# First convolution's stage: the nodes' leaky rows are made on VectorE, and their own rows are added there from SBUF

## The reference

```
x = _layernorm(x + _L0_gnn_ref(x, edge_index, ...))                   # graph convolution, twice, 64 -> 128 -> 64
x = _layernorm(x + _L1_gnn_ref(x, src, dst, ...))                     # attention over the edges
x = _layernorm(x + _L2_gnn_ref(x, edge_attr_64, ..., edge_type_10))   # relations; ends as below
x = _layernorm(x + _L3_gnn_ref(x, src, dst, edge_attr_32, ...))       # messages and an update MLP
```

```
out = leaky_relu((nfeat + h_nb) @ res_fc_w.T, 0.01) + leaky_relu(nfeat * h_nb @ res_fc2_w.T, 0.01)
x   = layernorm(x + out)
```

## Time and profile before

| | |
|---|---|
| median of 3 runs | 4774.9 us (4772.15 to 4782.6) |
| profiled execution: its own time | 4780.41 us |
| profiled execution: span of the trace | 4778.7 us |
| granted TensorE clock, mean over the span | 0.884 |
| first convolution's stage in the span | about 859 to 1422 us, 98 turns |

### The profile page before, as it was taken

One profiled execution on the slowest core, in us unless ns is written; L12 is line 12 of the kernel. 1 busy time (PEld: TensorE's weight loads), 2 busy tenths in 40 slices (PEclk: granted clock), 3 DMA queues, 4 the chain that ended last, 5 costly groups with the idle time before them and its releaser, 6 DMA issues. The chain is left out here.

```text
span 4778.7 us, 78736 instructions
## 1 busy us (share of the span) xinstructions
PE 4088.1 (86%) x24119; PEld 2923.4 (61%) x24119; DVE 3215.4 (67%) x7115; ACT 1960.7 (41%) x3684; POOL 2801.5 (59%) x2859
## 2 busy tenths in 40 slices
PE   5989999799989999778996899898998666777776
PEld 1278888688877777668884555555555344444443
DVE  9967777667667888767776688888888433333332
ACT  0056666344444445324342155555555222222222
POOL 0066665576656666577762545455550377777777
PEclk9989999899999999855555989999998799888888
DMA  1089998799986676545543444444442222222221
GB/s 40 1 256 286 287 287 270 196 230 230 229 216 171 191 191 188 139 95 136 133 114 86 109 104 110 107 112 107 113 110 53 67 66 66 55 66 67 55 65 29
DMA packets 1127654, 649.03 MB, mean 136 GB/s; under 512 B 908912, under 2 KB 944313, under 8 KB 1127240
## 3 DMA queue, kind: packets, MB, share of 16 engines
q1 hardware_dynamic: 1039432, 555.85, 42.4%
q0 software_dynamic: 87808, 88.16, 9.3%
HBM read 384.70 MB, written 261.63 MB: 135 GB/s over the span
## 5 line engine op out<-in xcount | busy, mean ns | idle before, releaser
L2237 POOL DMA_INDIRECT r_got<-x_table,slot_idx x392 | 409.9, 1046 | 568.5 <-DVE r_masked L2470 340.0
L1089 POOL DMA_INDIRECT o_rows<-in_x_dram,dst_idx x392 | 369.9, 944 | 444.8 <-POOLq L348 242.0
L2552 POOL DMA_INDIRECT m_rows<-x_table,slot_idx x392 | 376.2, 960 | 223.9 <-issue 118.8
L2691 DVE TENSOR_TENSOR_SCAN m_both<-m_keep,m_both,m_rows_t 128x512 f32<-128x512 bf16 x97 | 124.1, 1280 | 545.2 <-PE m_rows_t L2614 545.2
L1541 POOL DMA_INDIRECT b_rows<-h_table,slot_idx x392 | 369.7, 943 | 206.9 <-issue 91.5
L1352 POOL DMA_INDIRECT a_got<-node_table,src_idx x392 | 375.5, 958 | 194.9 <-DVE a_conv L1488 57.4
L2336 PE MATMUL r_source_t<-r_masked,rel_pair 64*128 64x512 f32 x980 | 470.9, 626 | 0.0
L2338 PE MATMUL r_own_t<-r_masked,rel_pair 64*128 64x512 f32 x980 | 470.8, 626 | 0.0
L2560 POOL DMA_INDIRECT out_dram<-s_res,put_out x392 | 390.5, 996 | 135.7 <-issue 109.8
L2010 POOL DMA_INDIRECT t_got<-x_table,slot_idx x392 | 377.5, 963 | 144.8 <-issue 101.2
L2470 DVE SCALAR_TENSOR_TENSOR r_masked<-r_half,r_both_t 128x512 f32<-128x512 bf16 x490 | 301.0, 678 | 68.3 <-PE r_both_t L2321 68.2
(11 more groups left out here) (401 smaller groups left out, 11785.3 us busy)
## 6 DMA issues: line engine op xcount, KB each, us to landing
x_table<-n_res SPq DMA_DIRECT2D x196, 256.0 KB
n_rows<-x_table SPq DMA_DIRECT2D x196, 256.0 KB
x_table<-s_res SPq DMA_DIRECT2D x294, 128.0 KB
node_table<-n_wide SPq DMA_DIRECT2D x98, 272.0 KB, 3.9
h_table<-n_conv SPq DMA_DIRECT2D x98, 256.0 KB
x_table<-s_res SPq DMA_DIRECT2D x98, 256.0 KB
r_feats<-in_edge_attr_dram SPq DMA_DIRECT2D x390, 64.0 KB
n_rows<-in_x_dram SPq DMA_DIRECT2D x97, 256.0 KB
```

The source lines that it names most:

```text
L1089: nc.gpsimd.indirect_dma_start(out=rows[:, n % 4, t, :], out_offset=None, in_=x, in_offset=bass.IndirectOffsetOnAxis(ap=dst_idx[:, n * TIL ...
L2237: nc.gpsimd.indirect_dma_start(out=got[:, n % RING, t, :], out_offset=None, in_=x2_table, in_offset=bass.IndirectOffsetOnAxis(ap=slot_idx[ ...
L2552: nc.gpsimd.indirect_dma_start(out=rows[:, n % 4, t, 0:D], out_offset=None, in_=x3_table, in_offset=bass.IndirectOffsetOnAxis(ap=slot_idx[ ...
```

## The change

In the relations layer only (this stage):

- ScalarE no longer applies ReLU: `take` copies the projected rows from PSUM to a new SBUF tile `n_plain`. Its place in ScalarE's list is that of the old bend. The next projection now waits for this copy.
- VectorE makes the leaky rows: `leak`, one scalar_tensor_tensor max(0.01 y, y) of 128x512, from `n_plain` to `n_hidden`.
- TensorE's `sum_up` keeps one product per group, `cen_pair` with `n_hidden`. The products with `slope_pair` are gone.
- The node's own (already centred) row is added on VectorE: `join_rows` adds `n_rows` from SBUF to the sum in PSUM and writes `n_whole` in SBUF. Squares and the final scaling read `n_whole` instead of PSUM (`squares_joined`, `scale_joined`). Loads of rows now also wait until the block that last held the buffer was joined.
- VectorE's list is in another order.

```diff
         def project(self, pe, n):
             pe.wait_ge(self.copied[n], self.copied.done(n))
             if n >= 1:
-                pe.wait_ge(self.bent[n - 1], self.bent.done(n - 1))
+                freed = self.plain_made if self.layer == "relations" else self.bent
+                pe.wait_ge(freed[n - 1], freed.done(n - 1))
...
                     if self.layer == "relations":
-                        nc.tensor.matmul(to[:, pair(q)], rows_s[:, pair(q)], slope_pair[:, :, :].rearrange("k j d -> k (j d)"),
-                                         start=(q == 0), stop=False, skip_group_check=True)
-                        last = nc.tensor.matmul(to[:, pair(q)], hidden[:, pair(q)], bent_pair[:, :, :].rearrange("k j d -> k (j d)"),
-                                                start=False, stop=True, skip_group_check=True)
+                        last = nc.tensor.matmul(to[:, pair(q)], hidden[:, pair(q)], cen_pair[:, :, :].rearrange("k j d -> k (j d)"),
+                                                start=(q == 0), stop=True, skip_group_check=True)
                         continue
...
+        def take(self, act, n):
+            act.wait_ge(self.projected[n], self.projected.done(n))
+            if n >= 2:
+                act.wait_ge(self.bent[n - 2], self.bent.done(n - 2))
+            nc.scalar.activation(self.plain[:, n % 2, :], self.hidden_t[:, :], ACT.Copy).then_inc(self.plain_made[n], 1)
+
+        def leak(self, dve, n):
+            dve.wait_ge(self.plain_made[n], self.plain_made.done(n))
+            if n >= 2:
+                dve.wait_ge(self.summed[n - 2], self.summed.done(n - 2))
+            nc.vector.scalar_tensor_tensor(out=self.hidden[:, n % 2, :], in0=self.plain[:, n % 2, :], scalar=SLOPE, in1=self.plain[:, n % 2, :],
+                                           op0=ALU.mult, op1=ALU.max).then_inc(self.bent[n], 1)
...
-                    over_turns((bend, 3, BLOCKS), (squares_nodes, 2, BLOCKS), (roots_nodes, 2, BLOCKS), (bend_nodes, 1, BLOCKS),
+                    over_turns((bend, 3, BLOCKS), (squares_nodes, 2, BLOCKS), (roots_nodes, 2, BLOCKS), (take_nodes, 1, BLOCKS),
                                (copy_nodes, 0, BLOCKS))
...
-                    over_turns((powers_nodes, 2, BLOCKS), (scale_conv, 3, BLOCKS), (add_terms, 3, BLOCKS), (invert_nodes, 2, BLOCKS),
-                               (scale_nodes, 2, BLOCKS), (sum_up, 1, BLOCKS), (scale, 0, BLOCKS))
+                    over_turns((join_nodes, 2, BLOCKS), (scale_conv, 3, BLOCKS), (add_terms, 3, BLOCKS), (powers_nodes, 2, BLOCKS),
+                               (leak_nodes, 1, BLOCKS), (sum_up, 1, BLOCKS), (invert_nodes, 2, BLOCKS), (scale_nodes, 2, BLOCKS),
+                               (scale, 0, BLOCKS))
```

More of the change, by code:

```diff
@@ L821, in __init__ @@
                 self.hidden = sb(c, "n_hidden", [P, 2, 512])
-            if layer == "update":
+                self.plain = sb(c, "n_plain", [P, 2, 512])
+                self.plain_made = sig.get("rising")
+            if layer in ("relations", "update"):
                 self.whole = sb(c, "n_whole", [P, 2, ROWS, D])
@@ L846, in load @@
                 sp.wait_ge(self.turned[n - AHEAD], self.turned.done(n - AHEAD))
-            if n >= AHEAD and self.layer == "update":
+            if n >= AHEAD and self.layer in ("relations", "update"):
                 sp.wait_ge(self.joined[n - AHEAD], self.joined.done(n - AHEAD))
@@ L929, in sum_up @@
                 pe.wait_ge(self.bent[n], self.bent.done(n))
-            if self.layer == "update":
+            if self.layer in ("relations", "update"):
                 if n >= 2:
@@ L987, in bend @@
                     act.wait_ge(self.summed[n - 2], self.summed.done(n - 2))
[L988 to L992, removed]
+            nc.scalar.activation(self.hidden[:, n % 2], self.hidden_t[:, :, :], ACT.Relu,
+                                 bias=(b1_col if self.gcn else u_b1)[:, 0:1]).then_inc(self.bent[n], 1)
+        def take(self, act, n):
[9 more added lines that the diff above has]
+                                           op0=ALU.mult, op1=ALU.max).then_inc(self.bent[n], 1)
         def squares(self, act, n):
@@ L1445, in copy_nodes, with take_nodes @@
                         nodes.copy(act, n)
-                    def bend_nodes(n):
-                        nodes.bend(act, n)
+                    def take_nodes(n):
+                        nodes.take(act, n)
                     def squares_nodes(n):
-                        nodes.squares(act, n)
+                        nodes.squares_joined(act, n)
                     def roots_nodes(n):
                         nodes.roots(act, n)
-                    over_turns((bend, 3, BLOCKS), (squares_nodes, 2, BLOCKS), (roots_nodes, 2, BLOCKS), (bend_nodes, 1, BLOCKS),
+                    over_turns((bend, 3, BLOCKS), (squares_nodes, 2, BLOCKS), (roots_nodes, 2, BLOCKS), (take_nodes, 1, BLOCKS),
                                (copy_nodes, 0, BLOCKS))
@@ L1504, in scale_nodes, with leak_nodes, join_nodes @@
                     def scale_nodes(n):
-                        nodes.scale_rows(dve, n)
-                    over_turns((powers_nodes, 2, BLOCKS), (scale_conv, 3, BLOCKS), (add_terms, 3, BLOCKS), (invert_nodes, 2, BLOCKS),
-                               (scale_nodes, 2, BLOCKS), (sum_up, 1, BLOCKS), (scale, 0, BLOCKS))
+                        nodes.scale_joined(dve, n)
+                    def leak_nodes(n):
+                        nodes.leak(dve, n)
+                    def join_nodes(n):
+                        nodes.join_rows(dve, n)
+                    over_turns((join_nodes, 2, BLOCKS), (scale_conv, 3, BLOCKS), (add_terms, 3, BLOCKS), (powers_nodes, 2, BLOCKS),
+                               (leak_nodes, 1, BLOCKS), (sum_up, 1, BLOCKS), (invert_nodes, 2, BLOCKS), (scale_nodes, 2, BLOCKS),
+                               (scale, 0, BLOCKS))
             sig.end_phase()
```

## The result

The changed kernel takes 4825.95 us (median of 3 runs, 4825.89 to 4830.29) against 4774.9 us before: a ratio of 1.0104, 95% interval 1.0084 to 1.0123. It is slower by 51 us, which is clear of the 0.2% that can be told. Measured again beside the experiments, the ratio was 1.0108 (1.0091 to 1.0125).

The account below looks back on a forecast made before the run. TensorE bounds the kernel before at 5.49 us a turn; afterwards a VectorE-ScalarE chain sets 5.99. 97 x (5.99 - 5.486) = +49 us on the profiled 4780.4, less 5.5 for the median, gave 4825 us, range 4803 to 4855.

Parts of the forecast that it names:

- TensorE sets the pace before: Relations stage before the change: TensorE busy 500 of 500 us, its timeline filling the 5.49 us turn without a hole.
- The floors: Least turn after the change: TensorE 4.60 us, gathers 3.8 and something between them, transfers 5.0, VectorE 5.03; all below 5.49.
- The chain: VectorE and ScalarE hand work over twice per turn; VectorE waits 0.96 us before the leak, making the turn 5.99 us.
- TensorE can deliver: TensorE's sums reach VectorE at 4.84 us after the join's start, needed at 5.99; TensorE idles 1.4 us per turn.
- J: Start of the join on VectorE, from which the forecast counts times in a turn, in us.
- The sum: Relations stage: 97 turns x (5.99 - 5.486) = +49 us, giving 4825 us for the median of the runs.
- The rival in which VectorE's queue is full: Wait for the leak hidden, turn 5.03 us: -44 us, 4731; with transfers at 0.91 share, -10 us, 4765. Chance 0.08.
- The clock rival: TensorE's idle time lowers its clock to 1.2 GHz: +30 to +100 us more, 4855 to 4925. Chance 0.08.
- The rule on the most-contended engine: Take the engine with highest occupancy, TensorE at 500 of 500 us, as bottleneck and relieve it first; the change then pays.

Follow-up runs that it names:

- e5: Changed kernel with all sixteen passes on TensorE again, the own row counted twice in the result: 4831.25 us, against 4832.43 for the changed kernel beside it.
- e1: Changed kernel with the copy (`take`) moved ahead of the root in ScalarE's list: 4740.37 us, 0.991 of the kernel before.
- e3: Changed kernel with the copy (`take`) one place later in ScalarE's list, behind the copy of the transposed rows: 4914.28 us, ratio 1.0272 to the kernel before.
- e4: Changed kernel without the leak: ScalarE applies ReLU straight to `n_hidden`, the slope left out; join and eight passes stay: 4741.93 us, 0.991 of the kernel before.
- e7: Kernel before with only the leak moved to VectorE: no join, sixteen passes, squares and scaling from PSUM: 4780.45 us, ratio 0.9998 to the kernel before.
- e2: Changed kernel with the scan moved ahead of the leak in VectorE's list: 4769.98 us, 0.997 of the kernel before.
- e6: Changed kernel with the copy (`take`) behind the copy of the transposed rows and sixteen TensorE passes, own row counted twice: 4888.34 us, ratio 1.0226 to the kernel before.

## Why the prediction was right

The forecast was 4825 us, the chance of slower 0.88, and the time is 4826 us. Step by step:

- **TensorE sets the pace before, and its queue is full.** e5 is the reverse test for after: with the sixteen passes back the time is the same, so after the change TensorE is off the path.
- **The floors are all below 5.49.** Right. VectorE's 5.03 us with no wait was measured as 5.01 in e1. The gathers' 3.8 us "and something between them" was too low a floor: back to back they take 5.0 us a turn in e1. It changed nothing here, since that too is under 5.49 and 5.99.
- **The chain.** From the join, predicted against the trace after: `n_power` 1.40 and 1.39, root 2.12 and 2.10, copy 2.33 and 2.30, leak 2.96 and 2.91, next join 5.99 and 6.01. The order decides, not the amount: e1 takes the chain apart with nothing removed and gains 94 us over the changed kernel, and e3 lengthens it. Neither half of the change does harm by itself: e4 (join, no leak) is faster than the kernel before, e7 (leak, no join) is level with it. Two small errors cancel, which is luck: the way to the leak was 0.05 shorter, and the leak to the next join 0.07 longer, most of it the step from the cast to the join, 0.14 in place of 0.08.
- **TensorE can deliver.** Its sums start at J + 3.66 (predicted 3.74). The projection is through 0.57 us after the join's start (1164.39 - 1163.82), not 1.4 as I wrote; 4.64 + 0.84 + 1.08 - 5.99, from the terms there and the earlier trace rows, is 0.57 as well. The copy wants it at 2.30, so nothing hangs on it.
- **The sum.** +49 us was forecast and +51 measured. 4780.4 + 48.9 - 5.5 is 4824 and not 4825, so the agreement within 1 us is in part luck; the turn, 5.99 against 6.01, is the fair comparison. Of these the stage has all: `a_terms` runs from 888.5 to 1468.1 now and from 889.8 to 1418.5 before, 50.9 us more.
- **The rival in which VectorE's queue is full** is not what happened, but it is what the change could have been: e1. There my upper end was wrong. I held that transfers at their present share of 0.91 would hardly let a turn go under 5.4; e1 and e4 run at 0.99. A share of 0.91 under a full TensorE was demand, not a limit.
- **The clock rival** did not come about with gaps of 1.15 us a turn, and did with 1.64 (e3). That part of the text was open. Its price in e3, 36 turns of 97 longer by 0.87 us, is 0.32 us in the mean turn, at the low end of the 0.3 to 1 us that I gave.
- **The rule on the most-contended engine** (the Trainium skill, Perfetto Trace Analysis, "Identifying the Most-Contended Engine") named TensorE rightly for the kernel before. That section of the Trainium skill makes an exception that I left out: for TensorE it does not go by the busy share of the matmuls but by their arithmetic rate or the busy share of the weight loads. By the latter TensorE leads as well, with 404.66 of 500 us against VectorE's 350. Relieving it paid only in e1, e2 and e4, in which no chain of over 5.49 us takes its place. The Trainium skill's sentence on feeding matmuls back to back (Perfetto Trace Analysis, "Matmul Optimizations") agrees with e3 and e6, at a granted clock of 0.90 and 1.00; it gives no figure by which e3 and the changed kernel, at 1.00 with a gap of 1.15 us, could have been told apart.

Not settled: whether the transfers or GpSimd's gathers are the floor of 5.0 us that e1 and e4 come to.

## What to carry to other kernels

When work is taken off the full engine, write down for one turn the order of each other engine's queue, and follow one instruction round the loop until it meets itself: a hand-over that goes to and fro twice in a turn adds up even when no engine is full. Busy shares and sums of work show only the floor. An instruction whose data are there, queued behind one that waits for another engine, is the first thing to move: here the copy ahead of the root turned +51 us into -43. Then look which loop comes next: the same eight passes that were free in e5 cost 8 us in e6, where the copies wait for TensorE.

## What the runs showed of the hardware

- The granted TensorE clock held at 1.00 with an idle time of 1.15 us in each turn of 6.01, and fell to 1.2 GHz for parts of the stage (mean 0.90) with one of 1.64 us in turns of 6.5. Eight more passes a turn brought it back to 1.00 with a gap of 0.83 us in turns of 6.58, and the kernel with more work was 24 us faster.
- The 16 DMA engines sustained a share of 0.99 at 253 GB/s over 450 us in e1, and VectorE's busy share was 0.986 at the same time. The busy share followed the demand: share times turn is 5.0 us at turns of 5.49 (0.91), 6.01 (0.84), 5.34 (0.94, e2) and 5.01 (0.99).
- GpSimd's indirect gathers of this stage start 1.25 us apart when nothing holds them up (359 in 450 us in e1), each lasting 0.95 us.
- The same scalar_tensor_tensor from SBUF took 0.69 us in this stage and 0.68 in the relation phase.
